# A decoder layer on one core: constant rows brought by transfer, four splits on VectorE, the feed-forward's first and last block in halves, and a new order of steps

## The reference

```python
x = x + self_attention(layernorm(x))        # softmax(q k^T / 4, causal) v, then Wo
x = x + cross_attention(layernorm(x), ctx)  # 77 keys, no mask
def act_fake_quant(x, clip):
    scale = sigmoid(clip) * max(abs(x)) / 127
    return clip(round(x / scale), -128, 127) * scale
xq = act_fake_quant(layernorm(x), clip_x)
h = act_fake_quant(silu(xq @ Wg_q.T) * (xq @ Wu_q.T), clip_down)
x = x + h @ Wd_q.T
```

## Time and profile before

| | us |
|---|---|
| median of 3 runs (lowest, highest) | 1051.85 (1050.81, 1053.42) |
| time of the profiled execution | 1059.1 |
| span of the profile of that execution | 1057.4 |
| PE busy | 905.4 (86%) |
| DVE busy | 716.3 (68%) |
| ACT busy | 611.8 (58%) |
| POOL busy | 363.6 (34%) |
| mean granted PE clock | 0.925 |

### The profile page before, as it was taken

One profiled execution on the slowest core, in us unless ns is written; L12 is line 12 of the kernel. 1 busy time (PEld: TensorE's weight loads), 2 busy tenths in 40 slices (PEclk: granted clock), 3 DMA queues, 4 the chain that ended last, 5 costly groups with the idle time before them and its releaser, 6 DMA issues. The chain is left out here.

```text
span 1057.4 us, 16929 instructions
## 1 busy us (share of the span) xinstructions
PE 905.4 (86%) x5859; PEld 449.9 (43%) x5863; DVE 716.3 (68%) x1413; ACT 611.8 (58%) x1114; POOL 363.6 (34%) x377
## 2 busy tenths in 40 slices
PE   2889999799899999999998989999997478667656
PEld 1534344264435443644453436444353334433234
DVE  7688776567677838677678286777714874379764
ACT  1426775545576576456766654567864145247594
POOL 7821343242421065333201652243112320047424
PEclk9979999999999999999999999999998776769877
DMA  4320123820221411112204111122006021021026
GB/s 151 114 79 26 46 65 68 113 65 34 91 75 32 159 38 56 46 61 75 83 30 160 41 58 39 61 80 81 25 22 196 6 79 40 40 100 60 1 80 199
DMA packets 79723, 75.97 MB, mean 72 GB/s; under 512 B 18984, under 2 KB 73896, under 8 KB 79640
## 3 DMA queue, kind: packets, MB, share of 16 engines
q1 hardware_dynamic: 74632, 71.36, 22.0%
q10 hardware_dynamic: 3456, 2.94, 0.9%
q0 software_dynamic: 1552, 0.58, 0.6%
HBM read 22.43 MB, written 13.13 MB: 34 GB/s over the span
## 5 line engine op out<-in xcount | busy, mean ns | idle before, releaser
L672 ACT ACTIVATE probs<-psum 128x512 f32<-128x512 f32 (+1 forms) x608 | 311.9, 577 | 183.1 <-PE psum L862 180.7
L1027 DVE CUSTOM_DVE_ANT_0 junk<-psum,mask 128x640 bf16<-128x640 f32 (+3 forms) x256 | 252.9, 1022 | 56.6 <-PE psum L827 54.8
L592 POOL TENSOR_SCALAR_AFFINE_SELECT probs<-probs 128x512 f32<-128x512 f32 x128 | 81.8, 642 | 391.3 <-ACT probs L672 391.1
L862 PE MATMUL psum<-q_stack,k_stack 98*128 98x512 bf16 (+3 forms) x768 | 185.5, 332 | 8.7 <-DMA q_stack<-max_rows 4.2
L887 PE MATMUL psum<-probs,v_sb 128*17 128x512 f32 (+3 forms) x1536 | 157.5, 491 | 3.0 <-POOL probs L592 2.7
L1023 DVE TENSOR_REDUCE rowmax<-psum 128x4 f32<-128x512 f32 (+2 forms) x96 | 97.5, 1045 | 78.0 <-PE psum L821 77.3
L827 PE MATMUL psum<-k_stack,q_stack 96*128 96x512 bf16 (+3 forms) x512 | 128.8, 346 | 5.5 <-DVE rowmax L1027 3.6
L862 PEld LDWEIGHTS psum<-q_stack,k_stack 98*128 98x128 bf16 x768 | 62.8, 98 | 137.6 <-ACT probs L672 80.9
L787 PE MATMUL psum<-xnT,wT 128*128 128x512 f32 x192 | 93.9, 628 | 0.3 <-ACT xprobs L677 0.3
L714 PE MATMUL psum<-wT,xnT 128*128 128x256 f32 x384 | 88.0, 388 | 0.2 <-DVE rowmax L1023 0.2
L714 PEld LDWEIGHTS psum<-wT,xnT 128*128 128x128 f32 x384 | 74.1, 196 | 11.1 <-issue 0.8
(11 more groups left out here) (155 smaller groups left out, 1264.4 us busy)
## 6 DMA issues: line engine op xcount, KB each, us to landing
q_stack<-q_parts SPq DMA_DIRECT2D x192, 64.0 KB, 2.6
k_stack<-k_parts SPq DMA_DIRECT2D x192, 64.0 KB, 2.6
xq_stack<-xq_parts SPq DMA_DIRECT2D x192, 64.0 KB, 2.6
xn<-in_x SPq DMA_DIRECT2D x8, 512.0 KB, 5.5
res<-in_x SPq DMA_DIRECT2D x4, 1024.0 KB, 9.2
resid_hbm<-res SPq DMA_DIRECT2D x8, 512.0 KB, 2.6
resid<-resid_hbm SPq DMA_DIRECT2D x8, 512.0 KB, 4.7
out<-o_sb SPq DMA_DIRECT2D x8, 512.0 KB, 3.2
```

Source lines behind the costliest of these rows:

```text
L592: nc.gpsimd.affine_select(out=tile, in_=tile, compare_op=ALU.is_ge, fill=0.0, base=0, pattern=[[0, GH], [1, P]], channel_multiplier=-1).th ...
L672: nc.scalar.activation(probs[n % 2][:, heads * k:heads * k + heads, 0:cols], bank_a(s)[:, 0:heads * cols].rearrange("p (h n) -> p h n", h= ...
L862: last = nc.tensor.matmul(bank[:, cols * n:cols * n + cols], k_stack[:, slot, h, P * j:P * j + P], q_stack[:, slot, half, h, q0 - HALF * h ...
L1027: nc.vector.tensor_tensor_reduce(out=junk[D_STEPS.place(s) % 2][:, 0:keys], in0=bank_d(s)[:, 0:keys], in1=m.mask[:, T - keys:T], scale=1.0 ...
```

## The change

Six things change.

1. POOL no longer fills `v_sb`, the ones rows and `xprobs`. It fills one tile `ones_row` of 2 x 128 bf16, and two DMAs on SP spread it over the rows of `k_stack` and `xk_stack`. DVE fills only the columns of ones of `v_sb` and of the context's values.
2. The q and k pieces of batch 0 with `c` = 0 (four steps) are split by DVE instead of POOL (`quick`), with the fp32 rest in `y_nat`.
3. In the feed-forward ACT rounds block 0 of the input, as soon as the scale is known (`x_known`), ahead of the tables of scales.
4. In the last block of the first loop DVE makes its products before it takes the maximum of the block ahead.
5. The second loop: block 0 is rounded, cut and multiplied in two halves of three tiles. `BACK` goes from 4 to 2: ACT subtracts on two tiles, DVE on four. In the last block PE finishes two token tiles and then the other two, DVE scales each half and adds the residual itself, and each half is stored by its own DMA.
6. `PICKS` is another string of the same 1915 steps.

```diff
+def quick(s):
+    return s[1:4] == (0, 0, 0)
...
 PICKS = (
-    "pppppppkppppppppvkkpkppppppqqpppmqmmmmmkmmqmmmmmmqqmsssmsmsmsssmvmssmvsmmvvmkmpvmmmpppvsssqmsmpmkkssqmsp"
+    "pppppppkpppkkkpppkqqvppkmpmmpppmmmppppmmpqqmqmmmmmmmmsssmmsssmmvmsssmsmvsvvkqmmppvqqmvssmssmmssmssmvmsms"
...
+                    if b == 0:
+                        sp.wait_ge(ones_done, 3)
+                        sp.dma_start(k_stack[ROWS:ROWS + SHIFT_ROWS, :, :, :].rearrange("p s h (a n) -> p (s h a) n", n=P),
+                                     ones_row[:].unsqueeze(1).to_broadcast([SHIFT_ROWS, 2 * GH * TT, P])).then_inc(ones_in, 16)
+                        sp.dma_start(xk_stack[ROWS:ROWS + SHIFT_ROWS, :, :].rearrange("p h (b n) -> p (h b) n", n=S),
+                                     ones_row[:, 0:S].unsqueeze(1).to_broadcast([SHIFT_ROWS, H * B, S])).then_inc(ones_in, 16)
...
-                nc.gpsimd.memset(v_sb[:], 1.0).then_inc(ones_done, 1)
+                nc.gpsimd.memset(ones_row[:], 1.0).then_inc(ones_done, 1)
                 pool.wait_ge(ones_done, 3)
                 pool.wait_ge(mask_done, 1)
-                nc.gpsimd.memset(k_stack[ROWS:ROWS + SHIFT_ROWS, :, :, :], 1.0).then_inc(ones_done, 1)
-                nc.gpsimd.memset(xk_stack[ROWS:ROWS + SHIFT_ROWS, :, :], 1.0).then_inc(ones_done, 1)
-                pool.wait_ge(ones_done, 5)
-                nc.gpsimd.memset(xprobs[:], 1.0).then_inc(ones_done, 1)
-                pool.wait_ge(ones_done, 6)
...
             nc.vector.memset(psum[:, 7, :], 0.0)
+            nc.vector.memset(v_sb[:, :, :, D:VW], 1.0)
+            nc.vector.memset(xv_all[:, :, :, D:2 * D], 1.0)
...
+                if s[0] in ("q", "k") and quick(s):
+                    parts, left = parts_of(s)
+                    n = QUICKS.upto(s)
+                    dve.wait_ge(*a_emptied(s))
+                    nc.vector.tensor_tensor(left, left, parts[:, 0, :], ALU.subtract).then_inc(quick_rem, 1)
+                    dve.wait_ge(quick_rem, n)
+                    nc.vector.tensor_copy(parts[:, 1, :], left).then_inc(quick_mid, 1)
+                    dve.wait_ge(quick_mid, n)
+                    nc.vector.tensor_tensor(parts[:, 2, :], left, parts[:, 1, :], ALU.subtract).then_inc(quick_low, 1)
...
-    MINE, BACK = 3, 4
+    MINE, BACK = 3, 2
...
+            act.wait_ge(x_known, 1)
+            nc.scalar.activation(xr[0][:], block_input(0), ACT.Identity, scale=small[:, XINV],
+                                 bias=magic[:, 0:1]).then_inc(x_first, 1)
...
+            for half in HALVES:
+                nc.scalar.activation(hr[0][:, half, :], hidden[:, 0, half, :], ACT.Identity, scale=small[:, HINV],
+                                     bias=magic[:, 0:1]).then_inc(first_rounded, 1)
...
             for n in range(NB):
-                if n == NB - 1:
-                    largest(n - 1)
                 products(n)
-                if 0 < n < NB - 1:
+                if n:
                     largest(n - 1)
...
+            for k, half in enumerate(HALVES):
+                dve.wait_ge(first_rounded, k + 1)
+                nc.vector.tensor_scalar(hq[0][:, half, :], hr[0][:, half, :], -MAGIC, None, ALU.add).then_inc(first_back, 1)
+                dve.wait_ge(first_back, k + 1)
+                nc.vector.tensor_scalar(hq[0][:, half, :], hq[0][:, half, :], QMAX, -QMAX - 1.0, ALU.min,
+                                        ALU.max).then_inc(first_done, 1)
...
+            for k in range(2):
+                here = o_sb[n % 2][:, 2 * k:2 * k + 2, :]
+                dve.wait_ge(last_down, k + 1)
+                nc.vector.tensor_tensor(here, m.psum[:, 2 * (n % 4) + k, :].rearrange("p (t c) -> p t c", c=C),
+                                        dscale[:, :].unsqueeze(1).to_broadcast([P, 2, C]), ALU.mult).then_inc(last_scaled, 1)
+                dve.wait_ge(last_scaled, k + 1)
+                nc.vector.tensor_tensor(here, here, resid[n % 2][:, 2 * k:2 * k + 2, :], ALU.add).then_inc(last_done, 1)
```

More of the change, by code:

```diff
@@ L421, in parts_of, with split_end @@
             tile = xq_parts[:] if layer else (q_parts if kind == "q" else k_parts)[:, c]
-            return tile[:, :, half * HALF:half * HALF + HALF], rem[SPLITS.place(s) % 4]
+            here = tile[:, :, half * HALF:half * HALF + HALF]
+            if quick(s):
+                return here, y_nat[:].rearrange("p t c -> p (t c)")[:, HALF * QUICKS.place(s):HALF * QUICKS.place(s) + HALF]
+            return here, rem[SPLITS.place(s) % 4][:]
+        def split_end(s):
+            return (quick_low, QUICKS.upto(s)) if quick(s) else (low_done, SPLITS.upto(s))
         def span(part):
@@ L495, in _ @@
                     (b, g, _), slot = HOLDS[n][0], n % 2
[L496 removed]
+                    sp.wait_ge(*split_end((which, 0, b, g // 2, half)))
                     if last_reader(n, (which, half)):
@@ L559, in _ @@
                     nc.gpsimd.tensor_tensor(xk_parts[c][2], xk_rem, xk_parts[c][1], ALU.subtract).then_inc(xlow, 1)
-                if s[0] in ("q", "k"):
+                if s[0] in ("q", "k") and not quick(s):
                     parts, left = parts_of(s)
@@ L658, in _ @@
                         bias = m.bias_t[:, 0 if which == "q" else 1, c:c + 1]
-                    if SPLITS.place(s) >= 4:
+                    if not quick(s) and SPLITS.place(s) >= 4:
                         act.wait_ge(low_done, SPLITS.place(s) - 3)
                     nc.scalar.activation(parts[:, 0, :], bank_a(s), ACT.Identity, bias=bias)
-                    nc.scalar.activation(left[:], bank_a(s), ACT.Identity, bias=bias).then_inc(a_free, 1)
+                    nc.scalar.activation(left, bank_a(s), ACT.Identity, bias=bias).then_inc(a_free, 1)
                 if s[0] == "mT":
```

148 lines of the change are left out of this document (88 added, 60 removed).

## The result

| | before | after |
|---|---|---|
| median of 4 runs, us (lowest, highest) | 1052.12 (1050.81, 1053.42) | 1039.78 (1035.36, 1041.25) |
| time of the profiled execution, us | 1059.1 | 1038.55 |
| span of its profile, us | 1057.4 | 1036.7 |
| mean granted PE clock | 0.925 | 0.941 |

The account below looks back on a forecast made before the run. PE's own work was taken to bound 76 to 800 us, chains of waits the stages around it. Terms 2 + 6.5 - 5.2 + 1.3 + 3.6 + 3.5 = 11.7 us off 1051.85 gave 1040.2, range 1031.5 to 1049.5.

Parts of the forecast that it names:

- Start: Up to the first scores of group 1: fills go, splits move to DVE; 2 us gained, between 7 gained and 3 lost.
- the slow rival: Rival E: PE's wait near 27 us brings half clock over the interleaved projections; 6 us slower, 1058; chance 0.05.
- Middle: 76 to 800 us: PE's 5.70 us wait for key stack pieces and its clock cost go; 6.5 us gained.
- Last batch: Up weights' transposes ahead of the first cross scores wait for DVE, so maxima turn later; 5.2 us lost, 3 to 7.
- Feed-forward, start: ACT rounds block 0 before the tables, so the first gate matmul comes at 938.1 instead of 939.38; 1.3 us gained.
- End of the first loop: DVE's products and last maximum follow without a gap in the feed-forward's first loop; 3.6 us gained, 2 to 4.
- Second loop: Down loop: halves shorten first and last block, period about 5.1 us; 3.5 us gained, 0 to 9.
- B: Down loop: DVE and POOL don't hinder each other, ACT's 4.0 us sets the period; 5.5 us more, 1034.7; chance 0.13.
- C: Rest of the order string wins 8 us more of PE's 38 idle ones; 1032; chance 0.12.
- D: The order's wins come to nothing: stack wait returns elsewhere, start even; 1048.6; chance 0.20.
- E: Start: PE waits for DVE's splits near 27 us, then half clock until the maxima's turn; 6 us slower, 1058; chance 0.05.

Follow-up runs that it names:

- a_old_tail: The changed kernel with the old order of steps from the last cross-attention's norm on: 1032.23 us, ratio to before 0.9801.
- a_kx_late: The changed kernel with the context's first key projection moved behind the first query and key projection: 1043.71 us, ratio to before 0.9897.
- a_old_string: The changed kernel with the old `PICKS` string, all other parts kept: 1056.26 us, ratio to before 1.0028.
- a_old_pool_split: The changed kernel with the old `PICKS` string and all splits on POOL again: 1043.32 us, ratio to before 0.9897.
- b_sp_moved: The kernel before with three steps of SyncE's list moved (residual's load, two stores of context keys and values): 1042.98 us, ratio to before 0.9929.

## Why the prediction was right, point by point

The forecast was 1040.2 us, the median is 1039.78. The sum is right within what the runs can tell, and so are the places and signs of its terms: the waits on the fills, at the stacks and for the up weights went or came as said. That it hit to 0.4 us is luck. The interval of the measured gain runs from 10.7 to 16.9 us, the terms were mostly too small by the traces, and I had taken 0.3% as what a measurement can tell, where the kernel before alone spreads over 17.6 us. By the ratios the parts add up: 8.7 for the feed-forward, 3.2 for the string and 2.1 for the constants make 14.0, with 13.8 measured for all.

**Start, forecast 2 us gained.** Measured 4.0 to 5.2 at the first marks and 3.3 from 124 us on. All signs came: 0.17 us, PE at 10.99, the context's wait until 16.81. The first score came at 35.06 instead of 37 to 38, and the clock did not fall between 27 and 52 us, so the slow rival had nothing to stand on here. The price of a split was near (1.7 taken, 1.8 to 2.6 measured), but the step that put the splits in as a gain of 1.4 and 2.8 us isn't borne out by the totals: on DVE or POOL they give the same time with this string, within the intervals. The full clock that I counted on from the turn on did not last either: it is 0.50 from 56 to 64 us now, where it was 0.50 from 52 to 64 before. And I costed string and splits apart, though they hang together: what stands behind the split on DVE decides between nothing and 13 us.

**Middle, forecast 6.5 us gained.** The place and mechanism were right. The size was short: the lead grows by 11.8 us between 164 and 216 us. Beside the wait of 5.7 us there were 2.0 us of waiting for a maxima transfer at 175 us and a second stretch at half clock behind it, both in the trace before and not in my sum. From 216 to 789 us, where I had put nothing, this profile gives 2.7 us back. That is the execution's and not the order's: by the same marks the eight other profiles with the new string in the middle change by -0.1 to +3.1 us there.

**Last batch, forecast 5.2 us lost.** Measured: 5.2 in the comparison with a_old_tail and 5.1 between the marks (14.2 to 9.0). By the kernel's total it costs 7.1, with an interval of 1 to 13, so the total neither adds to the 5.2 nor takes from it.

**Feed-forward, start, forecast 1.3.** From DVE's first fill after the barrier (932.27, 920.87) to the gate it was 7.1 and is 5.3 us: 1.8. The clip behind the rounding on ACT takes 0.43 us instead of 1.15.

**End of the first loop, forecast 3.6.** From the gate to the second loop 65.46 became 60.71 us, and 61.5 to 61.7 in half of the other kernels: 3.8 to 4.8. No gap in front of the last maximum, as foretold.

**Second loop, forecast 3.5.** 2.7 in this profile, 2.4 to 2.6 in three others with the same second loop, and 0.2 to 0.8 in a_kx_late, a_old_string and a_old_pool_split; in the first two the wait for the last residual is 5.1 and 5.0 instead of 2.9 us. I had the period at 5.1 and it is 5.29; the rule of the Trainium skill ("SBUF — State Buffer", section "SBUF: two separate sides") taken in full gave 5.3 and a term of 2.3, and the trace agrees with it: POOL's addition, begun 0.2 us after the longer cut, takes 3.20 us and ends 2.2 us after the cut, about the 2.34 that it takes alone, and the clip ends 0.8 us after the addition. What I left out was the residual's load: in the last block DVE waits for it ahead of its scaling, where before POOL's addition had only DVE to wait for (2.34 us). How much of that wait reaches the end depends on PE. In this profile PE ends its last matmul at 1032.13 and DVE scales the second half at 1032.66, so 0.5 us at most; in a_kx_late it is 1033.88 and 1038.22, so over 4 us. The loop became slower per block and was paid back by the halves at its start.

These marks add up to 20.7 us where the medians differ by 12.3. The rest is mostly the profiled execution of before, 7 us above its median with a mean clock of 0.925; that of after lies 1.2 below its own. The stack wait stands in every profile with the old transfers, but how long PE runs at half clock does not, and the sum took both from that one execution.

**The rivals.** B needed a period of 4.0 us and had 5.29. C needed 8 us more from the rest of the string; behind the stack wait's surroundings the nine profiles show between 2.7 lost and 3.1 won. D, the order's wins come to nothing, is refuted at the stack wait by b_sp_moved; by D the string alone would have cost the 5.2 us of the last batch, and it won 3.2. E did not occur with the new string. With the old one DVE's splits did hold PE up, for 8.6 and 6.3 us; the clock of 0.50 behind the first wait, from 32 to 36 us with PE busy for 2.96 us, can have added 1.5 us, so the loss was the waits and not the half clock that E feared.

## What to carry to other kernels

An engine's list is served in order: before work is moved to a faster engine, look at what stands behind it there and when its operands come; here four splits of 1.8 to 2.6 us cost 13 us under one order and nothing that could be measured under another. Look on a DMA queue for large or many-rowed transfers between a producer's pieces and their reader; three moved steps were worth 7.5 us by the ratio. The whole new string alone is no better (3.2, with overlapping intervals): its trace wins 12 us at the same place, but is 4 us behind from the start and loses 5 in the last batch. In a loop on VectorE and GpSimd count the operation that the other engine holds up: giving GpSimd's share to the busier engine made the loop 0.7 us shorter per block.

## What the runs showed of the hardware

The same program differs by up to 17.6 us between executions on one chip (29 runs of the kernel before, 1043.59 to 1061.17 us). Over its 70 runs on four chips the mean granted PE clock goes with the time: 0.946 for the fastest (1041.94), 0.925 to 0.927 for the five slowest, a correlation of -0.86 and 7.7 us for each 0.01. In the profiles much of the difference arises in the last batch, from 850 to 900 us, where PE is busy for 7 to 10 of 10 us and is granted 2.4 GHz for some stretches and 1.2 for others: a_kx_late came there 1.4 us ahead of the changed kernel and left it 2.0 us behind, with a clock of 0.50 to 0.84 in the five windows of 10 us where the changed kernel has 0.61 to 0.99. Whether a small shift ahead of this stage decides which stretches get the full clock, or only the execution does, one profile of each kernel can't tell. A gain of a few microseconds ahead of such a stage can't be read from the end of the span. Marks ahead of it can tell it; twelve runs of each kernel still left an interval of 6 us.
